# A graph-attention kernel: first source chunk normalised in two halves, statistics, low keys and value products reordered in the opening stage

## What is computed

```python
h  = maximum(layernorm(x), 0)                         # source rows
hs = layer_norm(h) * ln1_scale + ln1_bias             # masked by node
ht = layer_norm(h_target) * ln1_scale + ln1_bias      # target rows
q, k, v = (ht@Wq + bq)/sqrt(32), hs@Wk + bk, hs@Wv + bv
logits = where(adj != 0, q @ k.T, -1e30)              # per head, 2048 x 2048
attn = softmax(logits) @ v @ Wo + bo
y  = layer_norm(ht + attn) * ln2_scale + ln2_bias
out = x + y + gelu(y @ W1) @ W2
```

## Time and profile before

| | us |
|---|---|
| three executions | 499.80, 499.89, 501.54 |
| their median | 499.89 |
| the profiled execution, device time | 502.69 |
| its span, first to last instruction | 500.8 |
| PE busy in the span | 477.0 (95%) |
| DVE busy | 416.5 (83%) |
| ACT busy | 376.4 (75%) |
| mean granted TensorE clock | 0.987 |

### The profile page before, as it was taken

How to read it: one execution, slowest core, us unless ns; L and a number is a source line. 1 busy time by engine, 2 the same in 40 slices (tenths; PEclk the granted TensorE clock), 3 DMA queues, 4 the chain that set the end, 5 groups by cost and what they waited for, 6 DMA issues and landing times.

```text
span 500.8 us, 10602 instructions
## 1 busy us (share of the span) xinstructions
PE 477.0 (95%) x4364; PEld 245.4 (49%) x4364; DVE 416.5 (83%) x616; ACT 376.4 (75%) x455; POOL 309.9 (62%) x153
## 2 busy tenths in 40 slices
PE   3899979999999999999999999999999799999995
PEld 1466633333433343333433343333345688888884
DVE  5788579999999999999999999998997577565252
ACT  4786978998988998988998998999994370727150
POOL 2000008995998999999999998999999300000000
PEclk9899998999999999999999999999999899999998
DMA  8997689822633674222763300160000100202021
GB/s 254 250 192 115 125 247 403 297 43 44 211 58 55 68 172 80 43 45 48 82 171 66 64 3 3 36 178 2 1 1 3 45 21 23 84 2 84 0 85 45
DMA packets 53231, 46.94 MB, mean 94 GB/s; under 512 B 35454, under 2 KB 46108, under 8 KB 52668
## 3 DMA queue, kind: packets, MB, share of 16 engines
q1 hardware_dynamic: 50672, 37.30, 28.0%
q0 software_dynamic: 2480, 8.92, 10.7%
q10 hardware_dynamic: 28, 0.01, 0.0%
HBM read 31.93 MB, written 14.81 MB: 93 GB/s over the span
## 4 chain that ended last, share of the span: by engine, by line
PE 60%; DVE 16%; issue 13%; POOL 5%; ACT 4%; DMA 1%; DVEq 0%; POOLq 0%
PE acc L1316 13%; PE slot L1301 13%; DVE probs L971 10%; PE acc L1334 6%; PE slot L1416 3%; PE slot L1415 3%; PE slot L1414 3%; PE acc L1429 3%; PE acc L1431 3%; PE acc L1430 3%; PE slot L1214 3%; POOL added_up L527 3%; PE slot L1232 2%; PE slot L1367 2%; DVE stats L812 1%
## 5 line engine op out<-in xcount | busy, mean ns | idle before, releaser
L971 DVE SCALAR_TENSOR_TENSOR probs<-maskT,slot 128x1024 f32<-128x1024 uint16 x256 | 298.3, 1217 | 8.3 <-PE slot L1301 7.8
L713 ACT ACTIVATE probs<-probs 128x1024 f32<-128x1024 f32 x256 | 267.0, 1057 | 25.8 <-DVE probs L971 7.4
L527 POOL TENSOR_TENSOR added_up<-added_up,probs 128x1024 f32<-128x1024 f32 x96 | 226.7, 2401 | 1.2 <-ACT probs L713 1.0
L1316 PE MATMUL acc<-probs,V 128*32 128x512 f32 x1024 | 137.2, 608 | 1.0 <-ACT probs L713 1.0
L1334 PE MATMUL acc<-probs,ones 128*32 128x256 f32 x1024 | 77.1, 379 | 0.0
L1334 PEld LDWEIGHTS acc<-probs,ones 128*32 128x32 f32 x1024 | 33.3, 110 | 72.8 <-issue 71.2
L1301 PE MATMUL slot<-q_hi,k_hi 32*128 32x512 f32 x512 | 64.7, 496 | 3.8 <-DVE probs L971 3.5
L524 POOL TENSOR_TENSOR added_up<-probs 128x1024 f32<-128x1024 f32 x16 | 38.0, 2395 | 31.0 <-ACT probs L713 20.5
L1301 PEld LDWEIGHTS slot<-q_hi,k_hi 32*128 32x128 f32 x512 | 24.6, 182 | 62.1 <-DVE probs L971 55.3
L770 ACT ACTIVATE g_full<-slot 128x512 f32<-128x512 f32 x32 | 19.3, 602 | 46.9 <-issue 30.9
L1301 PE MATMUL slot<-q_lo,k_hi 32*128 32x512 f32 x512 | 52.0, 392 | 0.0
(11 more groups left out here) (130 smaller groups left out, 489.0 us busy)
## 6 DMA issues: line engine op xcount, KB each, us to landing
adj_raw<-in_adj POOLq DMA_DIRECT2D x16, 512.0 KB, 5.8
xs<-in_x SPq DMA_DIRECT2D x4, 512.0 KB, 7.0
htn<-in_L_gnn_h_target SPq DMA_DIRECT2D x4, 512.0 KB, 6.8
ht_saved<-htn SPq DMA_DIRECT2D x1, 2048.0 KB, 7.6
k_hi_saved<-k_hi SPq DMA_DIRECT2D x1, 2048.0 KB, 10.6
k_lo_saved<-k_lo SPq DMA_DIRECT2D x1, 2048.0 KB, 14.1
v_saved<-V SPq DMA_DIRECT2D x1, 2048.0 KB, 9.3
inverse<-inverse_saved SPq DMA_DIRECT2D x8, 256.0 KB
```

The lines of the kernel that those rows point to most:

```text
L527: nc.gpsimd.tensor_tensor(added_up[:, pair], added_up[:, pair], at(i), ALU.add).then_inc(added, 1)
L713: nc.scalar.activation(p, p, ACT.Exp).then_inc(exped, 1)
L971: nc.vector.scalar_tensor_tensor(out=probs[:, u % RING], in0=m, scalar=-HALF_EDGE, in1=slot[u % SLOTS][:], op0=ALU.add, op1=ALU.min).then_ ...
L1316: mm = pe.matmul(acc[HD * j:HD * j + HD, 0, :], V[:, i, h * HD:(h + 1) * HD], probs[:, (PAIRS * k + j // 2) % RING, j % 2, :], start=(i == 0),
```

## The change

1. SP loads source chunk 0 as two halves of two tiles (`x_in_half`), so one more transfer is issued ahead of chunk 1.
2. DVE and ACT treat chunk 0 in two halves (`centre_half`, `rectify_half`, `half_stats`, `root_half`, `half_scale`, `normalise_half`). The small operations are issued once for each half. `centre(1)` moves from second place in DVE's queue to behind `test_nodes()`.
3. `source_stats(1)` goes behind `source_affine(0)`, `keys_lo(0)` ahead of `centre(2)`, and `keys_lo(1)` ahead of `centre(3)`. `keys_lo(2)` and `keys_lo(3)` stay.
4. On ACT `rectify(1)` and `mask_beta(1)` come behind `mask_beta(0)`; the root of chunk `c+1` stands between the two groups of `keys_hi(c)`; `values_out(0)` comes ahead of the two activations into `bv_wide`.
5. On PE `values(c)` is split in two halves of two tiles, one ahead of and one behind `turn_source(c+1)` (for the last chunk `turn_target(0)`). Two identity products stand ahead of the first transposes instead of three, and two more behind them.

```diff
-WARM = 3
+WARM = 2
+HALF = 2
...
-            for c in range(2):
-                sp.dma_start(xs[:, rows_of(c), :], x_rows[:, rows_of(c), :]).then_inc(x_in[c], 16)
+            for h in range(HALF):
+                sp.dma_start(xs[:, half_of(h), :], x_rows[:, half_of(h), :]).then_inc(x_in_half[h], 16)
+            sp.dma_start(xs[:, rows_of(1), :], x_rows[:, rows_of(1), :]).then_inc(x_in[1], 16)
...
-            rectify(0)
-            rectify(1)
-            source_root(0)
-            normalise_source(0)
+            rectify_half(0)
+            rectify_half(1)
+            root_half(0)
+            root_half(1)
+            normalise_half(0)
+            normalise_half(1)
             mask_beta(0)
+            rectify_chunk(1)
+            mask_beta(1)
+            keys_hi(0, [0])
             source_root(1)
-            mask_beta(1)
+            keys_hi(0, [1])
             normalise_source(1)
-            keys_hi(0)
-            rectify(2)
             mask_beta(2)
+            rectify_chunk(2)
+            values_out(0)
...
-            values_out(0)
+            keys_hi(1, [0])
             source_root(2)
-            keys_hi(1, [0])
+            keys_hi(1, [1])
             normalise_source(2)
-            keys_hi(1, [1])
-            rectify(3)
             mask_beta(3)
+            rectify_chunk(3)
...
+            def half_stats(h):
+                variances(half_of(h), h * TILES // HALF, HALF_A * h, TILES // HALF)
+
+            def half_scale(h):
+                dve.wait_ge(rooted_h, h + 1)
+                scale_rows(half_of(h), h * TILES // HALF, HALF * HALF_A + 6 * h, TILES // HALF)
...
-            centre(0)
-            centre(1)
+            centre_half(0)
+            centre_half(1)
+            half_stats(0)
+            half_stats(1)
             dve.wait_ge(columns_turned, 1)
...
-            source_stats(0)
             dve.wait_ge(nodes_made, 1)
-            source_scale(0)
+            half_scale(0)
+            half_scale(1)
             test_nodes()
+            centre(1)
+            source_affine(0)
             source_stats(1)
-            source_affine(0)
             source_scale(1)
+            keys_lo(0)
             centre(2)
             source_affine(1)
-            keys_lo(0)
             source_stats(2)
             source_scale(2)
+            keys_lo(1)
             centre(3)
             source_affine(2)
-            keys_lo(1)
             source_stats(3)
             source_scale(3)
             target_stats(0)
             source_affine(3)
             keys_lo(2)
...
-            for n in range(WARM):
-                pe.matmul(acc[:, 1, :], ident[:], ident[:, None, :].to_broadcast([P, TILES, P]), start=True, stop=True)
+            warm_up(WARM)
             turn_source(0)
+            warm_up(2)
             keys(0)
+            values(0, 0)
             turn_source(1)
-            values(0)
+            values(0, 1)
             keys(1)
+            values(1, 0)
             turn_source(2)
-            values(1)
+            values(1, 1)
             project_rest()
             keys(2)
+            values(2, 0)
             turn_source(3)
-            values(2)
+            values(2, 1)
             keys(3)
+            values(3, 0)
             turn_target(0)
-            values(3)
+            values(3, 1)
```

More of the change, by code:

```diff
@@ L195, in graph_attention @@
         x_in = [sem(f"x_in{c}") for c in range(NCH)]
+        x_in_half = [sem(f"x_in_half{h}") for h in range(HALF)]
         ht_in = [sem(f"ht_in{c}") for c in range(NCH)]
@@ L809, in _, with row_stats @@
         def _(dve):
-            def row_stats(src, t0, into, into0, signal, done):
-                for t in range(TILES):
+            def row_stats(src, t0, into, into0, signal, done, tiles=TILES):
+                for t in range(tiles):
                     nc.vector.bn_stats(stats[:, t, :], src[:, t0 + t, :]).then_inc(signal, 1)
-                dve.wait_ge(signal, done + TILES)
-                for t in range(TILES):
+                dve.wait_ge(signal, done + tiles)
+                for t in range(tiles):
@@ L828, in inverse_root, with centre_rows @@
                                                ).then_inc(signal, 1)
                 dve.wait_ge(signal, done + 4)
[L831 to L834, removed]
+            def centre_rows(ts, done, tiles):
+                row_stats(xs, ts.start, moments, ts.start, norm_x, done, tiles)
                 nc.vector.tensor_scalar(shift[:, ts, :], moments[:, ts, 0:1], -1.0, None, ALU.mult
@@ L836, in centre, with centre_half @@
                                         ).then_inc(centred, 1)
[L838 to L843, removed]
+            def centre_half(h):
+                dve.wait_ge(x_in_half[h], 16)
+                centre_rows(half_of(h), 2 * TILES // HALF * h, TILES // HALF)
+            def centre(c):
+                dve.wait_ge(x_in[c], 16)
+                centre_rows(rows_of(c), 2 * TILES * c, TILES)
@@ L844, in source_stats, with variances @@
+            def variances(ts, into0, base, tiles):
+                dve.wait_ge(rectified, ts.stop)
+                row_stats(xs, ts.start, second, into0, norm_h, base, tiles)
                 nc.vector.tensor_scalar(spread[:, ts, :], moments[:, ts, 1:2], EPS, EPS * EPS, ALU.mult, ALU.add
                                         ).then_inc(norm_h, 1)
-                dve.wait_ge(norm_h, base + 2 * TILES + 1)
-                nc.vector.tensor_tensor(spread[:, ts, :], spread[:, ts, :], second[:, :, 1:2], ALU.add
+                dve.wait_ge(norm_h, base + 2 * tiles + 1)
+                nc.vector.tensor_tensor(spread[:, ts, :], spread[:, ts, :], second[:, into0:into0 + tiles, 1:2], ALU.add
@@ L1223, in keys, with values @@
                 project(slot[1], wk, hsT[c % 2], k_projected, x_affine, c)
-            def values(c):
-                if c == 0:
+            def values(c, half):
+                if half:
+                    pass
+                elif c == 0:
                     pe.wait_ge(wv_in, 16)
@@ L1229, in values @@
                     pe.wait_ge(v_out, c)
-                for t in range(TILES):
+                for t in range(half * TILES // 2, (half + 1) * TILES // 2):
                     for d in range(DC):
@@ L1233, in values @@
                                        start=(d == 0), stop=(d == DC - 1))
-                mm.then_inc(v_projected, 1)
+                if half:
+                    mm.then_inc(v_projected, 1)
             def queries(c):
```

65 lines of the change are left out of this document (46 added, 19 removed).

## The result

| | before | after |
|---|---|---|
| median of 20 executions each | 501.39 us | 500.02 us |
| lowest to highest | 499.49 to 503.79 | 498.06 to 501.95 |
| the profiled execution, device time | 502.69 | 500.01 |
| its span | 500.8 | 498.3 |
| mean granted clock in it | 0.987 | 0.990 |

The ratio after to before is 0.9962, with a 95% interval of 0.9946 to 0.9979. The change makes the kernel 0.4% faster, and the interval leaves out 1. I had forecast no change: 499.9 against 499.89. The time itself came out at my number; the time of the kernel before did not. Its median over 20 executions is 501.39, 1.5 us above that of the three I had read.

What follows compares the result with a forecast made beforehand. PE, busy 95%, was taken as the bound, with gains only from earlier first scores: 68.9 to 67.3, 1.6 us; since runs without the clock fall lose 1.65 less, the median changes +0.1, to 499.9 us, range 498.1 to 501.4.

Steps and rivals of the forecast that it cites:

- what that means for the median: Whole kernel: runs at 499.8 lack the clock fall at 16.9 costing 1.65 us, so the change gives +0.1 us, 499.9.
- in no median run: Opening, near 17 us: the forecast case, no clock fall in the median run and clock high in time; chance 0.45.
- in every run: Rival: the fall near 17 us is in every run before, spread comes from near 390; saves 1.6, 498.3; chance 0.22.
- The layouts: DVE, ACT and PE queues laid out up to first scores: 68.9 before against 69.47 traced, 67.3 after; only differences used.
- The first half's landing: Opening load: first half of chunk 0 lands at 4.25 us, between 3.1 and 4.94; the second at 4.95.
- Part 1: Halved load of chunk 0: halves land at 4.25 and 4.95 us; chunk 1 about 0.5 us later, hidden.
- Part 2: Chunk 0 in halves on DVE and ACT: `hsT` starts at 14.5 instead of 16.26, 1.8 us earlier, DVE's queue last.
- Part 3: Identity products around chunk 0's transposes: second pair fills PE's 1.74 us wait free; keys(0) 3.4 us ahead, 1.6 by clock.
- Part 4: Chunks 1 and 2: PE waits 1.1 and 1.0 us for tiles; keys(1) 2.3 us ahead, keys(2) 2.5.
- Part 5: Split values at chunk 3: PE waits 1.2 us for `keys_lo(2)` ahead of keys(3), leaving it 1.6 us ahead.
- The slower rival: Clock not up behind chunk 0's first transposes: 501.0, or 502.7 if keys(0) run low too; chance 0.15, 0.03 for the whole.
- Later dips: Clock falls at 75 and 390 us met differently: up to 1.7 us either way, 498.2 or 501.6; 0.18 together with load.

## Why the prediction was wrong

**The step that failed: what that means for the median.** I took three times in two groups 1.7 apart and gave the gap to the one fall that I had costed, so the median run had no fall near 17. Three of four traces have it. The median of the three, 499.89, stood for one of the four fastest executions of 20; the median of the 20 is 501.39, in the group whose traces have one of the two falls. The fall near 390, which I had named as the rival source of the spread, comes and goes too (429.7 against 431.3 to 431.5 us behind the scores). My argument against it, that a longer empty stretch should make that fall the steadier, didn't hold. Both the forecast ("in no median run") and the rival ("in every run") were too simple: it is in some. The sentence on the Trainium skill ("TensorE: Matmul & The Clock Gate", Part 1: The HAM clock gate), that the monitor of activity runs free of the kernel's start so that the point of a change differs from run to run, agrees with the four traces, in which the fall near 17 is there or not. I used it to excuse the inference, where it ought to have warned that each of the falls is a draw of its own.

A number that I had spoke against the step. The traced execution has 502.69, and 1.65 less is 501.04, not 499.9: the one fall left 1.1 us of the distance unexplained.

That 499.9 came out all the same is luck. I built it on the executions near 499.8, which by the groups above have neither fall. The changed kernel's executions with a mean clock of 0.995 or more take 498.1 to 498.9, but for one. Its median of 500.02 is higher because most of its executions lose more clock than these; the traced one, of 500.01, loses 1.71 near 390.

How often the kernel before has the fall stays open. The traces say 3 in 4. The times say less: the difference of the medians is 1.4 and of the means 1.8 us (501.67 against 499.87); with 0.8 for the order (below), 0.6 to 1.0 is left for the fall; at 1.65 us a fall that is 4 to 6 executions in 10. The kernel with only the two products, which moved by 0.6, says some 4 in 10. These shares are estimates, and too low if a fall that is spared near 17 makes that near 75 longer. Of the eight traces without a fall near 17 four lose 3.4 us near 75, of the six with one only one does, and it costs 0.5 to 0.8 us behind the scores (431.8 against 431.3, 430.5 against 429.7). With so few traces this can't be settled.

**The term that was mis-sized: the order's own gain.** With no fall, I had the scores of before at 67.25 and of after at 67.3, so the reordering was worth -0.1. The third trace of before and the one with only the two products have 67.89 and 67.82; after has 66.96 and 67.21. The change gains 0.6 to 0.9 with no fall in either, some 0.8 on average. Two terms were off:

- *The layouts.* I wrote that mine came out 0.1 to 0.4 early for each chunk of the kernel before, 0.6 at the scores, and took the error to be common to both. It wasn't: for after my layout, at 67.3, was 0.1 to 0.3 late. No run shows why the handoffs that I left out cost less in the new order.
- *The first half's landing.* DVE starts at 3.73 (3.70 in the second trace), taken was 4.25 between bounds of 3.1 and 4.94. The row for 256 KB (2.2) gave 3.1, and measured is 2.8 to 2.9 from issue. The 0.7 us that I added behind the bytes was right. The moment of the bytes was not: I read 3.5 from the kernel before, and with the load in halves 256 KB have moved by 3.0, by the slices of 0.15 us from 0 to 6 us of the changed kernel:

```profile
GB/s 0 1 0 0 0 0 0 0 0 0 0 0 7 123 205 198 198 246 348 352 324 318 386 375 355 185 82 157 157 219 232 307 348 335 348 328 369 362 403 266
```

**The other parts.**

- Part 1, chunk 1 "0.5 later": wrong, 3.6 later, and hidden as I said, by the new order. With `centre(1)` left in second place DVE waits 3.80 for it (the load alone).
- Part 2: forecast `hsT` at 14.5, 1.8 earlier; measured 13.80, 2.46 earlier, 0.5 of it by the landing. Right in kind: `centre(1)` in DVE's queue is what is last.
- Part 3: the pair costs nothing and keys(0) take 3.67 with no gap: right in the first trace; in the second keys(0) wait some 0.6 for it. What it is worth is in doubt: in two traces of the changed kernel without it the clock stays up.
- Part 4: keys(1) forecast at 24.1, measured 23.46; keys(2) 33.7 and 33.06. The 0.64 is there nearly from the start (keys(0) 15.25 and 14.70). The tile waits I expected ahead of the second value half, 1.0 to 1.1 us a chunk, show as transposes that take 1.82 instead of 1.04: 0.8.
- Part 5: wait of 1.2 forecast, 1.09 measured, in both traces. The run with the low keys further forward gives back 1.14. This was the best argued term, and it is also the defect of the change.
- The slower rival (clock late): not in the two traces of the change, where the second pair takes 1.88 for four records, which is full clock. The trace with chunk 0 whole has the low clock there. It has the same two products ahead of the transposes, and besides them a wait of 1.44 for the first tile; that this wait is the cause isn't shown.
- Later dips: the second loss of 1.7 near 75 is in several kernels without a fall at 17. It costs less than 1.7: 430.5 and 430.7 behind the scores against 429.7. Near there PE also waits for DVE, 1.88 us ahead of the second scores in the first trace of the changed kernel, and while it waits a low clock costs nothing; that this is the reason is argued and not shown.

## What to carry over

A fall of the clock that a trace shows is one draw: before giving a spread of times to it, count the other places where PE comes out of an empty stretch, take several traces of the same kernel, and don't read a median from three times. Splitting a group of products into filler work before and behind a turn opens a wait at every chunk where the buffer that the next group needs isn't freed sooner as well; read the last chunk as well as the first. An extra transfer ahead of others may make its own data come sooner and delay the next by far more than its issue.

## What the runs showed of the hardware

- One more transfer ahead, of the same bytes in all, moved the next one's landing from 5.1 to 8.2 us after its issue (8.4 with the load alone split). The cause is not settled; the bytes ahead of it are the same.
- With chunk 0 loaded in halves the first 256 KB had moved by 3.0 us of the span, where they had by 3.5 with the load whole.
- Granted clock is lost in pieces of 1.70 to 1.71 us, one or two in a row, at the same few places. Which of them occur differs between executions of one kernel; near 17 us it does so after the same idle time of 1.74 us.
- The small vectors, all but one of 1 KB and issued early, land between 7.23 and 8.89 us, and differ by over 1 us between two executions of one kernel. Only a quarter to a half of this reaches the first scores: 66.96 and 67.21 (landing 7.23 and 8.33), 66.75 and 67.41 (7.42 and 8.89).
